# A second softmax with the keys on the partitions: exact fp32-in-three-products attention and feed-forward block

## The reference, cut to what matters

```python
h = layernorm(x) * (1 + ca) + sa
Q, K, V = split(h @ c_attn_w + c_attn_b)
base_A = softmax(Q[:, :, :128] @ K[:, :, :128].T * SCALE)          # first softmax
cam = tanh((base_A @ V[:, :, :128]) * cam_gate) @ K[:, :, :128].T * (SCALE * layer_weight)
final_attn = softmax(Q @ K.T * SCALE + cam)                        # second softmax
x = x + ga * (final_attn @ V @ c_proj_w + c_proj_b)
h = layernorm(x) * (1 + cb) + sb
x = x + gb * (gelu(h @ proj1.T + b1) @ proj2.T + b2)               # feed-forward, 1024 hidden
```

## Time and profile before

| | before |
|---|---|
| median of 3 runs | 334.62 us (333.51 to 335.08) |
| span of the profiled execution | 331.2 us |
| PE matmul busy | 312.6 us (94%), 2004 instructions |
| PE weight load busy | 282.5 us (85%) |
| DVE busy | 228.1 us (69%) |
| ACT busy | 135.2 us (41%) |
| POOL busy | 117.8 us (36%) |

### The profile page before, as it was taken

The page is one execution under the profiler, slowest core; times in us unless marked ns, Lnnn a source line. Parts: engine busy times, 40 slices in busy tenths (PEclk is TensorE's granted clock), DMA queues, the critical chain, the costliest instruction groups (busy, mean ns, idle before and its releaser), DMA issues.

```text
span 331.2 us, 5156 instructions
## 1 busy us (share of the span) xinstructions
PE 312.6 (94%) x2004; PEld 282.5 (85%) x2004; DVE 228.1 (69%) x430; ACT 135.2 (41%) x227; POOL 117.8 (36%) x143
## 2 busy tenths in 40 slices
PE   2899999989999999899999999999999999989986
PEld 2789989877999998798889788888998999789885
DVE  4986688899774576897644689897564584881541
ACT  2455575545243344404503576644522344420400
POOL 2401221360653534844921032240023132842651
PEclk9999999999999999999999999999999999999999
DMA  6900100700000000010000000000000000001001
GB/s 241 370 24 9 25 2 1 255 0 0 2 0 2 0 4 0 0 34 32 2 32 32 1 3 2 0 0 2 0 2 0 2 0 2 1 0 55 11 18 49
DMA packets 7832, 10.04 MB, mean 30 GB/s; under 512 B 640, under 2 KB 6528, under 8 KB 7808
## 3 DMA queue, kind: packets, MB, share of 16 engines
q1 hardware_dynamic: 7808, 9.71, 8.6%
HBM read 7.35 MB, written 2.10 MB: 29 GB/s over the span
## 4 chain that ended last, share of the span: by engine, by line
PE 58%; DVE 19%; POOL 9%; issue 7%; ACT 5%; DMA 1%; SPq 0%; POOLq 0%; DVEq 0%
PE a_ps L185 11%; PE a_ps L187 10%; PE a_ps L186 10%; PE s_ps L185 6%; PE s_ps L187 6%; PE s_ps L186 6%; PE t_ps L875 5%; POOL pt_hi L334 5%; DVE nmax L608 4%; POOL x_all L341 3%; ACT prob L434 3%; DVE pt_lo L635 2%; PE t_ps L778 2%; DMA wmod_raw<-wmod 1%; DVE bst L539 1%
## 5 line engine op out<-in xcount | busy, mean ns | idle before, releaser
L426 ACT ACTIVATE pt_hi<-t_ps 128x512 fp32r<-128x512 f32 x64 | 34.9, 596 | 62.2 <-PE t_ps L875 62.1
L608 DVE TENSOR_REDUCE nmax<-s_ps 128x1 f32<-128x1024 f32 x32 | 39.0, 1218 | 17.6 <-PE s_ps L187 17.4
L306 POOL TENSOR_SCALAR prob<-prob,rinv 128x1024 f32<-128x1024 f32 x16 | 18.0, 1124 | 76.1 <-DVE rinv L612 76.1
L434 ACT ACTIVATE prob<-s_ps,nmax 128x1024 f32<-128x1024 f32 x32 | 35.7, 1117 | 20.4 <-DVE nmax L608 20.2
L635 DVE TENSOR_TENSOR pt_lo<-f32s,pt_hi 128x512 fp32r<-128x512 f32 x32 | 29.6, 943 | 17.4 <-POOL pt_hi L334 17.4
L602 DVE TENSOR_TENSOR pt_lo<-t_ps,pt_hi 128x512 fp32r<-128x512 f32 x64 | 40.9, 679 | 0.0
L185 PE MATMUL a_ps<-w_hi,pt_hi 128*128 128x256 f32 x128 | 37.0, 289 | 2.8 <-DVE pt_lo L635 2.8
L185 PE MATMUL s_ps<-k_hi,q_hi 128*128 128x512 f32 x96 | 38.4, 400 | 0.8 <-ACT prob L434 0.8
L457 ACT ACTIVATE f32s<-s_ps,cols_sb 128x512 f32<-128x512 f32 x32 | 22.1, 690 | 39.2 <-PE s_ps L187 33.4
L187 PE MATMUL s_ps<-k_hi,q_lo 128*128 128x512 f32 x96 | 37.7, 393 | 0.0
L186 PE MATMUL s_ps<-k_lo,q_hi 128*128 128x512 f32 x96 | 37.5, 391 | 0.0
(11 more groups left out here) (116 smaller groups left out, 740.1 us busy)
## 6 DMA issues: line engine op xcount, KB each, us to landing
x_all<-x SPq DMA_DIRECT2D x4, 512.0 KB, 8.9
w_raw<-w_t SPq DMA_DIRECT2D x2, 1024.0 KB, 6.0
out<-x_all SPq DMA_DIRECT2D x16, 128.0 KB, 1.7
wmod_raw<-wmod SPq DMA_DIRECT2D x1, 1024.0 KB, 9.3
wmod_raw<-wmod SPq DMA_DIRECT2D x1, 512.0 KB, 4.7
wattn_raw<-w_attn SPq DMA_DIRECT2D x1, 512.0 KB, 6.1
wvt_raw<-wv_t SPq DMA_DIRECT2D x1, 256.0 KB, 7.1
wp_raw<-wp SPq DMA_DIRECT2D x1, 256.0 KB, 7.2
```

Source lines behind the costliest of these rows:

```text
L306: G.tensor_scalar(prob[:, u % 3, :], prob[:, u % 3, :], rinv[:, u:u + 1], 1.0, ALU.mult, ALU.mult).then_inc(pnorm_ready, 1)
L426: A(pt_hi[:, (u // 2) % 2, 4 * g:4 * g + 4, (u % 2) * P:(u % 2 + 1) * P], t_bank(b, "p", 2 * u + g)[:, :].rearrange("p (t n) -> p t n", n= ...
L434: A(prob[:, u % 3, :], s_ps[u % 2][:, :], ACT.Exp, bias=nmax[:, u:u + 1], accum_out=rsum[:, u:u + 1]).then_inc(exp_ready, 1)
L608: V.tensor_reduce(nmax[:, u:u + 1], s_ps[u % 2][:, :], AX.X, ALU.max, negate=True).then_inc(nmax_ready, 1)
```

## The change

1. **Second softmax with keys on the partitions.** The eight units of 128 queries become four blocks of 256 queries (`BLOCKS`, `QB`). `key_scores` puts 128 keys on the partitions and 256 queries in the columns, with the keys as weights: 48 matmuls of 256 columns a block, in all four banks of `s_ps`. The exponentials then lie as the value product needs them, and the 64 transposes of probabilities a batch are gone.
2. **The maximum.** DVE folds the four banks into one 128x512 tile (`block_max`), PE transposes it (`transpose_max`, four pieces), DVE reduces it (`block_shift`), PE spreads the negated maxima over the partitions (`spread_max`, two pieces), ACT copies them (`copy_shift`), DVE adds them to the four banks (`block_subtract`). ACT takes exponential and copy in pieces of 512 columns (`exp_block`).
3. **The sum** comes from the value product: v_hi gets a column of ones and one of zeros (`NVS`), two of the three matmuls of `attend` have 258 columns; `attn_gated` takes the reciprocal of that column.
4. **Low parts** of the exponentials: pieces 0 and 2 of a block on DVE, 1 and 3 on POOL (`block_low`).
5. **Order.** `cam_context` 2 and 3 stand between the first key scores and the second. `attend` 6 and 7 stand between `ffn_up` 3 and 4; the first half of `ffn_down` 0 and 1 stands ahead of `h_transpose` 6 and 7. `qk_project(1, 0)` stands ahead of batch 0's last four `ffn_down`, and an exponential of one column ends batch 0's ACT program.
6. **Gates' floor** on POOL, on each batch's own gate rows before they are spread by DMA (`floor_gates`, then four DMAs in place of two); `finish_consts` on POOL too. The high parts of the feed-forward weights move from POOL to ACT (`ffn_high`).

```diff
-UNITS = 2 * T
+NVS = NV + 2
+BLOCKS = T // 2
+QB = 2 * P
...
+        v_hi = sb("v_hi", [P, T, NVS], F32R)
+        v_lo = sb("v_lo", [P, T, NV], F32R)
...
-            late = {5 + 2 * p: [("ctx", p)] for p in range(T // 2)}
+            late = {5: [("ctx", 0)], 7: [("ctx", 1)]}
...
+            T_JOBS += [(b, "p", n) for n in range(2 * T)]
+            T_JOBS += [(b, kind, i) for i in range(BLOCKS - 1) for kind in ("m2t", "nmb")]
+            T_JOBS += [(b, "h", 4), (b, "m2t", BLOCKS - 1), (b, "h", 5), (b, "nmb", BLOCKS - 1), (b, "h", 6), (b, "h", 7)]
...
+            def block_low(b, i, j):
+                wait(pool, sthi_ready, b, 4 * i + j + 1)
+                G.tensor_tensor(pt_bank(pt_lo, i, j), est_bank(j), f(pt_bank(pt_hi, i, j)), ALU.subtract)\
+                    .then_inc(stlo_odd, 1)
...
+            def floor_gates():
+                pool.wait_ge(gate_copied, 1)
+                G.tensor_scalar(gate_sgn, gate_own, 0.0, -0.5, ALU.is_ge, ALU.add).then_inc(gate_sign, 1)
+                pool.wait_ge(gate_sign, 1)
+                G.tensor_tensor(gate_own, gate_own, gate_sgn, ALU.mult).then_inc(gate_abs, 1)
+                pool.wait_ge(gate_abs, 1)
+                G.tensor_scalar(gate_own, gate_own, 4.0, 0.5, ALU.mult, ALU.max).then_inc(gate_floor, 1)
+                pool.wait_ge(gate_floor, 1)
+                G.tensor_tensor(gate_own, gate_own, gate_sgn, ALU.mult).then_inc(gate_floor, 1)
...
+                for s in range(T):
+                    divide_by_sum(b, s)
+                    if b == 0 and s == 1:
+                        floor_gates()
+                    if b == 0 and s == 4:
+                        finish_consts()
+                for t in range(4):
+                    attn_const(b, t)
+                for i in range(BLOCKS):
+                    if i in (1, 2):
+                        attn_residual(b, 2 * i - 2)
+                        attn_residual(b, 2 * i - 1)
+                    if b == 0 and i == 3:
+                        split_ffn(7)
+                    block_low(b, i, 1)
+                    if b == 0 and i == 0:
+                        split_ffn(0)
+                    block_low(b, i, 3)
+                    if i == 2:
+                        inv_std(b, 2)
+                    if i == 0:
+                        for t in range(4, T):
+                            attn_const(b, t)
+                    if b == 0 and i < 3:
+                        for n in ((1,), (2, 3, 4), (5, 6))[i]:
+                            split_ffn(n)
+                attn_residual(b, 4)
                 attn_residual(b, 5)
                 for n in range(HC):
+                    if n == 4:
+                        attn_residual(b, 6)
+                        attn_residual(b, 7)
                     gelu_high(b, n)
+                    if n == 4:
                         inv_std(b, 3)
...
+            def copy_shift(b, i):
+                wait(act, nmb_psum, b, i + 1)
+                A(nmb_of(i), t_bank(b, "nmb", i)[:, 0:QB], ACT.Copy).then_inc(nmb_ready, 1)
+            def ffn_high(n):
+                src, hi, _ = ffn_part(n)
+                act.wait_ge(w1_in if n < 4 else w2_in, 16)
+                A(hi, src, ACT.Copy).then_inc(wffn_hi, 1)
+            def exp_block(b, i):
+                for j in range(4):
+                    wait(act, shift_ready, b, 4 * i + j + 1)
+                    A(est_bank(j), est_bank(j), ACT.Exp).then_inc(est_ready, 1)
+                    if j == 0 and i == 1:
+                        wait(act, ctx_psum, b, 4)
+                    if j == 0 and i >= 2:
+                        wait(act, pv_psum, b, 2 * (i - 1))
+                    wait(act, est_ready, b, 4 * i + j + 1)
+                    A(pt_bank(pt_hi, i, j), est_bank(j), ACT.Copy).then_inc(sthi_ready, 1)
+                    if b == 0 and i < 2:
+                        ffn_high(4 * i + j)
...
+                prob_high(b, T - 2)
+                prob_high(b, T - 1)
+                copy_shift(b, 0)
+                cam_tanh(b, 2)
+                for i in range(BLOCKS):
+                    exp_block(b, i)
+                    if i + 1 < BLOCKS:
+                        if i == 0:
+                            cam_tanh(b, 3)
+                        if i == 2:
+                            affine(b, 4)
+                            affine(b, 5)
+                        copy_shift(b, i + 1)
...
+                    qk_bias(b + 1, 0)
+                    A(lw_scr[:, :], lw_arg[:, :], ACT.Exp)
...
+            def block_max(b, i, j):
+                wait(dve, st_psum, b, 4 * i + j + 1)
+                if j == 0:
+                    V.tensor_copy(m2_of(i), s_bank(0)).then_inc(m2_ready, 1)
+                else:
+                    wait(dve, m2_ready, b, 4 * i + j)
+                    V.tensor_tensor(m2_of(i), s_bank(j), m2_of(i), ALU.max).then_inc(m2_ready, 1)
+            def block_shift(b, i):
+                wait(dve, m2t_psum, b, i + 1)
+                V.tensor_reduce(nmax_st[:, i % 2, :], t_bank(b, "m2t", i)[:, :].rearrange("p (a n) -> p a n", n=QB),
+                                AX.X, ALU.max, negate=True).then_inc(nmst_ready, 1)
+            def block_subtract(b, i, j):
+                wait(dve, nmb_ready, b, i + 1)
+                nmb = nmb_of(i).rearrange("p (a n) -> p a n", a=1).to_broadcast([P, 2, QB])
+                V.tensor_tensor(est_bank(j).rearrange("p (c n) -> p c n", n=QB),
+                                s_bank(j).rearrange("p (c n) -> p c n", n=QB), nmb, ALU.add).then_inc(shift_ready, 1)
+            def block_low(b, i, j):
+                wait(dve, sthi_ready, b, 4 * i + j + 1)
+                V.tensor_tensor(pt_bank(pt_lo, i, j), est_bank(j), f(pt_bank(pt_hi, i, j)), ALU.subtract)\
+                    .then_inc(stlo_even, 1)
...
+                prob_low(b, T - 2)
+                for j in range(4):
+                    block_max(b, 0, j)
+                prob_low(b, T - 1)
+                block_shift(b, 0)
+                for j in range(4):
+                    block_subtract(b, 0, j)
+                q_update(b, 2)
+                for i in range(1, BLOCKS):
+                    block_low(b, i - 1, 0)
+                    if i == 3:
+                        tile_stats(b, 2, 0)
+                        tile_stats(b, 2, 1)
+                    block_max(b, i, 0)
+                    if i == 3:
+                        tile_stats(b, 2, 2)
+                        tile_stats(b, 2, 3)
+                        half_stats(b, 2)
+                    block_low(b, i - 1, 2)
+                    block_max(b, i, 1)
+                    block_max(b, i, 2)
+                    if i == 3:
+                        norm_apply(b, 2)
+                    block_max(b, i, 3)
+                    block_shift(b, i)
+                    if i == 2:
+                        q_update(b, 3)
+                    if i == 3:
+                        h_split(b, 4)
+                        h_split(b, 5)
+                    block_subtract(b, i, 0)
+                    for j in range(1, 4):
+                        block_subtract(b, i, j)
+                    attn_gated(b, 2 * i - 2)
+                    attn_gated(b, 2 * i - 1)
+                block_low(b, BLOCKS - 1, 0)
+                block_low(b, BLOCKS - 1, 2)
+                for n in range(4):
+                    gelu_low(b, n)
+                attn_gated(b, T - 2)
+                tile_stats(b, 3, 0)
+                tile_stats(b, 3, 1)
                 attn_gated(b, T - 1)
+                tile_stats(b, 3, 2)
+                tile_stats(b, 3, 3)
+                half_stats(b, 3)
+                gelu_low(b, 4)
+                norm_apply(b, 3)
+                for n in range(5, HC):
                     gelu_low(b, n)
...
+            def key_scores(b, i):
+                wait(pe, qplo_ready, b, i + 1)
+                if i == 0:
+                    wait(pe, qklo_ready, b, 8)
+                n = slice(i * QB, (i + 1) * QB)
+                for j in range(4):
+                    if i == 0 and j % 2 == 0:
+                        wait(pe, exp_ready, b, T - 1 + j // 2)
+                    if i:
+                        wait(pe, shift_ready, b, 4 * (i - 1) + j + 1)
+                    for c in range(2):
+                        keys = slice((2 * j + c) * P, (2 * j + c + 1) * P)
+                        for k in range(EC):
+                            last = mm3(s_bank(j)[:, c * QB:(c + 1) * QB], k_hi[:, k, keys], k_lo[:, k, keys],
+                                       q_hi[:, k, n], q_lo[:, k, n], k == 0, k == EC - 1)
+                    last.then_inc(st_psum, 1)
+            def transpose_max(b, i):
+                wait(pe, m2_ready, b, 4 * i + 4)
+                t_free(b, "m2t", i)
+                for a in range(2):
+                    for c in range(2):
+                        last = nc.tensor.transpose(t_bank(b, "m2t", i)[:, (2 * a + c) * P:(2 * a + c + 1) * P],
```

(47 more changed lines are left out.)

292 lines of the change are left out of this document (139 added, 153 removed).

## The result

The changed kernel takes 335.22 us (median of 20 runs, 333.56 to 337.03), the kernel before 333.66 in the same series (20 runs, 332.17 to 335.19). The ratio is 1.0039, 95% interval 1.002 to 1.0057: a little slower, and inside the 0.5% that the prediction calls no change. Forecast were 331.3 and faster. The time lies inside the range, the sign is wrong.

A forecast was written before the change was run, and what follows sets the result against it. TensorE's (PE's) program was taken as the bound, with matmuls in flight for 94% of the span. 331.2 - 6.2 (work) - 5.1 (stalls going) + 8.0 (stalls coming) = 327.9 span, plus 3.4 gives 331.3 us; range 326 to 337.5.

The forecast's parts named there:

- PE's work: Second softmax on PE: four blocks a batch take 48.3 instead of 51.5 for eight units; 6.2 us gained over both batches.
- The wide matmul: Rival, chance 0.04, shared with moved pieces not moving: value-product matmuls of 258 columns cost half-way to 512, 14 more, 345.
- Stalls that go: PE waits removed: probability low parts 2.1, last gelu_low 1.0, batch 1's first exponential 0.9, mid feed-forward 1.1; 5.1 us gained.
- The fourth block: Last block of each second softmax: DVE has 15.2 of work against PE's 12.1, norm_apply priced 1.97; 2.6 lost a batch.
- The middle: Middle of the feed-forward: PE's loss of 3.7 over both batches shrinks to 2 x 1.3; 1.1 gained.
- Start of each second softmax: DVE, behind after a slow query update, delays the first transpose of maxima by 1.3 in each batch; 2.6 lost.
- q_update(3): Query update in DVE's third block, partly beside POOL's weight splits in batch 0 only; 0.2 lost.
- Floor of the gates and constants on POOL: Up to 7.8 of POOL work in batch 0's first softmax, covered by POOL's waiting: no cost; uncovered, 2 to 3.
- The offset of 3.4: Amount by which the median of the runs stands above the profiled span, added to 327.9 to give 331.3.
- The ring: Rival, chance 0.22: DVE or the chain from key scores to block_subtract bounds every block; 335.3 to 339.3, mostly no change.
- The stalls did stay away: Rival, chance 0.20: DVE's extra fourth-block work is hidden, costing only 1 a batch; 325.3, to 329.
- the fourth rival: Chance 0.09: DVE's and POOL's low parts block each other on the shared port, each DVE one costing 2.0; 344.

The follow-up runs named there:

- e7: The kernel before plus only the early first q/k projection of batch 1 and the early one-column exponential (table load): 330.8 us, ratio 0.9928 to the kernel before.
- e4: The changed kernel plus three unused two-input POOL subtractions in batch 1's fourth block, where batch 0 has its weight splits: 339.68 us, ratio 1.0169 to the kernel before.
- e5: The changed kernel with batch 0's POOL weight splits moved earlier, ACT's high parts in one run, attention constants after the query update: 329.67 us, ratio 0.9889 to the kernel before.
- e9: e5's kernel with gelu high parts earlier and constants last on POOL, gelu 5's low part before norm_apply on DVE: 327.63 us, ratio 0.9819 to the kernel before.
- e2: The changed kernel with POOL's four attention-constant additions waiting for the end of DVE's second query update: 334.14 us, ratio 1.0004 to the kernel before.
- e6: The changed kernel with all low parts of the second softmax's exponentials on DVE, none on POOL: 338.1 us, ratio 1.0155 to the kernel before.
- e8: The changed kernel with the old middle order: attend 6 and 7 ahead of ffn_up, each ffn_down whole: 346.26 us, ratio 1.0387 to the kernel before.

## Why the prediction was wrong, by its own steps

- **PE's work, 6.2 gained: right.** From cam_context 1's end to the feed-forward, the time without late starts fell from 60.2 to 57.2 in batch 0 and from 60.0 to 57.2 in batch 1, 5.8. A block takes 12.15 (235.80 to 247.95) where 12.08 were reckoned, since its matmuls stand 0.120 apart, not 0.1177. The wide matmul cost nothing, so that rival falls; at 0.1207 it is by the letter over the 0.12 that the prediction named as a sign of being wrong, and by less than a thousandth of a microsecond beyond the narrow one's 0.120.
- **Stalls that go, 5.1: 4.0 of it right.** The three waits for low parts, 2.1: gone from where they were (what came at unit 6 is counted below). The waits at 166.50 and 190.05, 1.9: that stretch is 1.82 shorter, and e7 shows it alone (2.4 by its ratio, 1.7 to 3.2 by its interval).
- **The step that failed: one price, 1.97, for norm_apply, wherever it stands.** That row, at 155.15 in the earlier trace rows, isn't of the second layer norm, as its heading has it: it is batch 1's first one, made during batch 0's feed-forward. The second layer norm's own two prices stood in the trace of before, without POOL beside it and beside POOL's conversions and additions:

```profile
117.55 1.38 DVE L557 TENSOR_SCALAR xn<-x_all,mv,rstd 128x256 f32<-128x256 f32 x4
...
134.34 2.80 DVE L557 TENSOR_SCALAR xn<-x_all,mv,rstd 128x256 f32<-128x256 f32 x4
```

  Measured were 1.37, 2.81 and, beside the weight splits, 3.86. It failed in two places.
  - **The fourth block, 2.6 a batch.** Batch 1 lost 1.5, less than forecast, batch 0 5.6: 0.25 + 3.25 + 0.33 + 0.38 and 1.4 of clock. The prediction placed the splits beside the query updates only. In the diff, parts 5 and 6 stand behind the last low part of block 2 and behind inv_std, and part 7 ahead of block 3's: exactly where DVE starts norm_apply. e4 puts this stall into batch 1, e5 takes it out of batch 0.
  - **The middle, 1.1 to be gained.** It is 0.8 worse than before. The layout by hand had 1.3 lost a batch and found 1.94, since norm_apply takes 2.8, with DVE's wait of 0.9 for the deviation ahead of it; e9 brings it down to 1.24. The late starts are then 3.9 against 3.7 before, so 0.6 of the 0.8 is something else: the 512-column matmuls of ffn_up stand 0.2333 apart (306.30 to 317.50, 48 of them), before 0.2273 (303.91 to 314.82). No run tells why. In the second half of the feed-forward, ffn_down gives most of it back (0.118 apart, before 0.120).

```profile
140.51 2.81 DVE L681 TENSOR_SCALAR xn<-x_all,mv,rstd 128x256 f32<-128x256 f32 x4 [0.92 <-POOL rstd L343]
```

- **The clock had no term.** The stall of 3.25 costs 4.6 with the fall of PE's granted clock behind it. The fall isn't the same in every execution: of the 20 runs of the changed kernel the mean granted clock was 1.0 in two (333.56 and 333.94 us, the time of the kernel before), 0.994 or 0.995 in 13 (334.9 in the mean) and 0.988 to 0.99 in five (336.6). The kernel before had 1.0 in most of its runs (e5's series: ten of eleven at 0.998 or more). So most of the 1.5 between the medians goes with the clock.
- **Start of each second softmax, 2.6:** 2.9 measured, but not where it was laid out. 0.6 a batch stands at the first transpose of maxima, where 1.3 was expected, and was work of POOL that could wait (e2). The largest piece, 0.96 in batch 0 and 0.47 in batch 1, stands ahead of unit 6's transposes, which the count had on time; the last 0.31 is unit 5's, below.
- **q_update(3), 0.2:** 0.55. Its first operation takes 1.54 beside a split, 0.48 in batch 1.
- **Floor of the gates and constants on POOL, nothing: nearly.** The third division of batch 0 came 3.7 after its reciprocal was ready, behind floor_gates, and PE didn't feel it. Unit 5's transposes are 0.31 late in batch 0 and on time in batch 1: beside finish_consts DVE's low part of the keys took 1.65, where it takes 0.69 alone.

```profile
50.37 1.65 DVE L707 TENSOR_TENSOR k_lo<-f32s,k_hi 128x512 fp32r<-128x512 f32 x1
```

  It is the same mechanism; that the two belong together is read from the order of events, no run separates it. Start-up differs by 0.4 between these two profiles and by over 1 among the others; what is between them isn't the change's to explain.
- **The offset of 3.4** was too large: the profiled run of the changed kernel took 335.48 with a span of 333.6, 1.9 above it. With 1.9 the same sum gives 329.8; that the forecast time lies within 4 of the measured one is in part luck.
- **The signs named.** Seen: 80 fewer transposes (48 for 128), the late starts at the first transpose of maxima, at h_transpose 4 and ahead of the first ffn_up, no table load in batch 1's first exponential. Of the signs of being wrong, key scores 3 was late in batch 0, single low parts of DVE took up to 1.78, and a division was late.
- **Rivals.** The groups of DVE's instructions in the changed kernel (line, count, busy us, mean ns):

```profile
L681 DVE TENSOR_SCALAR xn<-x_all,mv,rstd 128x256 f32<-128x256 f32 x32 | 17.0, 593 | 3.0 <-POOL rstd L343 3.0
L750 DVE TENSOR_TENSOR f32s<-s_ps,f32s 128x512 f32<-128x512 f32 x24 | 16.5, 688 | 2.3 <-PE s_ps L224 0.7
L766 DVE TENSOR_TENSOR pt_lo<-prob,pt_hi 128x512 fp32r<-128x512 f32 x16 | 16.1, 1014 | 0.5 <-ACT pt_hi L537 0.5
```

  The ring didn't become the bound: blocks two and three of batch 1 have no late start over 0.16. The low parts block each other where they meet (1.60 in each batch's last block, 0.68 alone), but they seldom meet: a DVE low part takes 1.01 in the mean, not 2.0, and e6, which separates them, is slower. The stalls did stay away in batch 1 in part (1.5 in place of 2.6). What decided was the mechanism of the fourth rival, at other operations than the rival named.

The missing 5.7, by terms: fourth block and q_update(3) 2.2, the middle 1.9, the work 0.4, the start 0.3, all against their forecasts; start-up 0.4. The remaining 0.5, most of it ahead of cam_context 1's end, is spread over starts too short to name, and stays open.

On the mechanism the Trainium skill ("SBUF — State Buffer", section "Who interferes with whom") was read too narrowly. It names two kinds of DVE operation that take the shared ports: those with two SBUF inputs, and copies, casts and operations with a scalar, which can enter a two-port mode from SBUF to SBUF. Only the first was weighed. No trace shows the mode, but the times agree with both kinds: norm_apply and the cast have one tensor input and go from 1.37 to 3.86 and from 0.29 to 1.24, while the folds, which read one bank of PSUM and one tile of SBUF, took 0.677 to 0.693 in all 24 cases, the two that stand beside the splits too (98.34 and 112.61).

## What to carry to other kernels

Before placing work on GpSimd, list what VectorE does in the same microseconds: each of its operations that stays within SBUF, even the shortest, can last until the GpSimd operation beside it ends, so put long GpSimd work beside VectorE's PSUM reads or its idle time, never beside a short chain that TensorE waits for. Price an operation by who stands beside it, batch by batch, when only one batch has the extra work. And when a pipeline's last stage gets longer (here 4.7 to 4.9 us stood open ahead of attend 6 in e8), count what work TensorE has to cover it before calling the reordering optional.
